# Talking-heads attention in pipelined pairs of tiles, and FiLM biases, on one Trainium2 core: the second mixing two pairs behind, three pairs of mixed scores, biases added by VectorE

## The reference, cut to what matters

```python
dots = jnp.einsum('bhid,bhjd->bhij', q, k) * scale        # k, v: 16 memory rows, then the tokens
dots = jnp.einsum('bhij,hk->bkij', dots, pre_proj)        # first mixing
dots = jnp.where(causal[None, None], neg, dots)
vk = lax.top_k(dots, 64)[0][..., -1:]
dots = jnp.where(dots < vk, neg, dots)
attn = jax.nn.softmax(dots, axis=-1)
attn = jnp.einsum('bhij,hk->bkij', attn, post_proj)       # second mixing
out = jnp.einsum('bhij,bhjd->bhid', attn, v)
return out.transpose(0, 2, 1, 3).reshape(b, n, h * d) @ Wo + bo
```

```python
scale_in, shift_in = jnp.split(c_t @ W_film_in + b_film_in, 2, axis=-1)
x = x * (1.0 + mod_gate * scale_in) + mod_gate * shift_in
y = s4d(x, ...)
scale_out, shift_out = jnp.split(c_t @ W_film_out + b_film_out, 2, axis=-1)
y = y * (1.0 + mod_gate * scale_out) + mod_gate * shift_out
```

## Time and profile before

| | us |
|---|---|
| Median of 3 timed runs (lowest, highest) | 4224.01 (4220.88, 4232.35) |
| The profiled execution, its own time | 4254.16 |
| Its span | 4252.3 |
| Busy in the span: PE, DVE, ACT, POOL | 3085.7, 2504.3, 1066.9, 967.3 |
| `l1_attention`, from the first search to the last reciprocal (1179 to 2713) | 1534 |
| `modulate` (from 2987.5) | 53 |
| `convolve` (3056.8 to 3233) | 176 |

### The profile page before, as it was taken

The page is one execution under the profiler, slowest core; times in us unless marked ns, Lnnn a source line. Parts: engine busy times, 40 slices in busy tenths (PEclk is TensorE's granted clock), DMA queues, the critical chain, the costliest instruction groups (busy, mean ns, idle before and its releaser), DMA issues. The chain is left out here.

```text
span 4252.3 us, 41618 instructions
## 1 busy us (share of the span) xinstructions
PE 3085.7 (73%) x12160; PEld 1887.1 (44%) x12160; DVE 2504.3 (59%) x7782; ACT 1066.9 (25%) x2741; POOL 967.3 (23%) x1212
## 2 busy tenths in 40 slices
PE   4747973997576777777677765443797855999997
PEld 2324552775343454455345444321233532555554
DVE  5994654551359989997999899568433141111112
ACT  1114531341133333333334332211001110111111
POOL 2540003002034544444444444200220000000000
PEclk6558986998657868767777866765898956999999
DMA  2000004554122122111212111000100003000000
GB/s 78 0 0 15 4 18 167 165 162 133 55 81 73 45 74 65 63 59 59 74 44 77 49 58 30 25 5 0 53 0 20 3 2 99 0 0 0 0 0 20
DMA packets 158964, 199.66 MB, mean 47 GB/s; under 512 B 30750, under 2 KB 133731, under 8 KB 158758
## 3 DMA queue, kind: packets, MB, share of 16 engines
q1 hardware_dynamic: 155686, 188.85, 14.1%
q0 software_dynamic: 3072, 8.39, 0.6%
HBM read 136.12 MB, written 61.08 MB: 46 GB/s over the span
## 5 line engine op out<-in xcount | busy, mean ns | idle before, releaser
L2058 DVE MATCH_REPLACE8 a_rest<-a_best,a_rest 128x416 f32<-128x416 f32 (+54 forms) x1308 | 605.0, 471 | 0.0
L2066 DVE MAX8 a_best<-a_rest 128x8 f32<-128x416 f32 (+54 forms) x1308 | 566.3, 475 | 0.0
L1736 PE MATMUL a_pmix<-a_rows,a_kpre 128*128 128x264 f32 (+41 forms) x528 | 244.7, 606 | 380.0 <-ACT a_mixed L1860 375.3
L2000 POOL TENSOR_SCALAR a_probs<-a_mixed,a_best 128x120 f32<-128x120 f32 (+12 forms) x208 | 285.7, 1373 | 377.5 <-DVE a_best L2070 354.2
L2843 DVE TENSOR_TENSOR e_hT<-e_act_out,e_pc 128x512 f32<-128x512 f32 x128 | 88.0, 687 | 478.4 <-ACT e_act_out L2834 472.8
L1736 PEld LDWEIGHTS a_pmix<-a_rows,a_kpre 128*128 128x128 f32 x528 | 123.7, 274 | 431.0 <-issue 423.6
L1745 PE MATMUL a_pat<-a_kp,a_probs 128*128 128x128 f32 x1344 | 261.2, 361 | 53.4 <-POOL a_kp L1962 48.5
L1745 PEld LDWEIGHTS a_pat<-a_kp,a_probs 128*128 128x128 f32 x1344 | 235.0, 262 | 126.7 <-POOL a_kp L1962 73.1
L2797 PE MATMUL e_ph<-xT,e_w 128*128 x512 | 244.4, 600 | 55.8 <-PEq L2760 46.7
L1726 PE MATMUL a_psc<-a_kT,branch 64*128 64x264 f32 (+3 forms) x640 | 234.8, 641 | 27.4 <-ACT a_stage L1827 26.6
L2814 PE MATMUL e_py<-e_w,e_hT 128*128 128x256 f32 x1024 | 254.4, 391 | 0.0
(11 more groups left out here) (448 smaller groups left out, 5608.0 us busy)
## 6 DMA issues: line engine op xcount, KB each, us to landing
f_w<-in_L_ffn_W SPq DMA_DIRECT2D x39, 1024.0 KB, 5.8
l_scores<-a_stage SPq DMA_DIRECT2D x32, 528.0 KB, 2.7
l_scores<-a_stage SPq DMA_DIRECT2D x32, 400.0 KB, 2.4
l_scores<-a_stage SPq DMA_DIRECT2D x32, 272.0 KB, 2.1
f0o_w<-in_L_ffn_W SPq DMA_DIRECT2D x8, 1024.0 KB, 12.5
sorted_x<-z_blank SPq DMA_DIRECT2D x1, 4992.0 KB, 17.1
f_xs<-sorted_x SPq DMA_DIRECT2D x39, 128.0 KB, 5.4
sorted_y<-f_ys SPq DMA_DIRECT2D x39, 128.0 KB, 5.7
```

The source lines that it names most:

```text
L1736: ins = pe.matmul(pmix[:, at, 0:hi - lo], kpre[:], rows[:, g % 4, lo:hi], start=True, stop=True)
L2000: ins = pool.tensor_scalar(p, x, best[:, a, LAST, 7:8], HIDE, ALU.is_lt, ALU.mult)
L2058: last[a] = signal(dve.match_replace(rest[:, a, 0:wd], best[:, a, q - 1, :], rows_of[a] if q == 1 else rest[:, a, 0:wd], GONE))
L2066: last[a] = signal(dve.max(best[:, a, q, :], rest[:, a, 0:wd]))
```

## The change

In `l1_attention`:

- `mixed` becomes a ring of six tiles (`DEEP`), three pairs; every index into it changes, and `mixed_out` waits for the mask of the tile six before.
- ACT's iteration k is now: mixed_out(k + 1) of both tiles, exps(k - 1), negated(k) of both, side(k), post_out(k - 2), products(k).
- `post`, `post_out`, `weights` and `invert` are now two pairs behind the search (k - 2); the loops of PE and ACT run one iteration longer. POOL's weights stand before the zeroing of `probs`.
- `heads` start one iteration later in a group, and the last iteration of a group has two of them; those of the very last group stand behind an extra iteration.
- The memory's values are no longer added by matmul. SP reads them from DRAM once a batch straight into `v`, after it has waited for two copies of values, and the first head product of a group waits for that (`mem_in`).

In the film stages the bias is read broadcast to 128 rows, `offset`, and made once into gate times bias, plus 1 in the left half. The one-row matmuls go, and one `scalar_tensor_tensor` of 512 columns (PSUM times gate plus `offset`) stands for the two `tensor_scalar` of 256.

```diff
-        return [(n, j) for j in range(8)] if s == 0 else []
+        return [(n, j) for j in range(8)] if s == 1 else []
...
-    return [(n, s)]
+    return [] if s == 0 else [(n, s - 1)] if s < STEPS1 - 1 else [(n, s - 1), (n, s)]
...
-        mixed = sb("mixed", [P, 4, KEYS1])
+        mixed = sb("mixed", [P, DEEP, KEYS1])
...
+                    if k >= 0 and (pos, s) == (1, 0):
+                        sp.wait_ge(sc_read, fills_to(("v", b, 1)))
+                        sp.dma_start(v[0:MEM, 0, :].rearrange("m (h d) -> m h d", h=H1),
+                                     d["L1_attn_mem_v"].rearrange("h m d -> m h d")).then_inc(mem_in, 16)
...
-                    if c == 0:
-                        ins = pe.matmul(out[:], G.ident[0:MEM, :], mv[:, half], start=False, stop=True)
...
-                        if k >= 1:
-                            post(2 * (k - 1) + a)
+                        if k >= 2:
+                            post(2 * (k - 2) + a)
...
-                for k in range(-1, PAIRS1 + 1):
-                    for a in range(2):
-                        if k >= 1:
-                            exps(2 * (k - 1) + a)
+                for k in range(-1, PAIRS1 + 2):
                     for a in range(2):
                         if k + 1 < PAIRS1:
                             mixed_out(2 * (k + 1) + a)
+                    for a in range(2):
+                        if 1 <= k <= PAIRS1:
+                            exps(2 * (k - 1) + a)
+                    for a in range(2):
                         if 0 <= k < PAIRS1:
                             negated(2 * k + a)
...
-                    if k >= 1:
-                        weights(k - 1)
...
-                        if q == min(rounds[0], TOP1 // 16) and pair >= 1:
-                            invert(pair - 1)
+                        if q == min(rounds[0], TOP1 // 16) and pair >= 2:
+                            invert(pair - 2)
+                invert(PAIRS1 - 2)
                 invert(PAIRS1 - 1)
...
+                sp.dma_start(offset[:], d["L1_xattn_b_film_in"].partition_broadcast(P)).then_inc(loaded, 16)
...
+                step(dve.tensor_scalar(offset[:], offset[:], gate[:, 0:1], None, ALU.mult))
+                step(dve.tensor_scalar(offset[:, 0:D], offset[:, 0:D], 1.0, None, ALU.add))
...
-                    dve.tensor_scalar(s1[:, i % 2], pw[i % 2][:, 0:D], gate[:, 0:1], 1.0, ALU.mult, ALU.add)
-                    ins = dve.tensor_scalar(h1[:, i % 2], pw[i % 2][:, D:2 * D], gate[:, 0:1], None, ALU.mult)
-                    ins.then_inc(emptied, 1)
+                    dve.scalar_tensor_tensor(film[:, i % 2], pw[i % 2][:], gate[:, 0:1], offset[:], ALU.mult, ALU.add
+                                             ).then_inc(emptied, 1)
...
-        pe.matmul(out[:], cT[:, k, i * P:(i + 1) * P], w[:, k, :], start=(k == 0), stop=False)
-    return pe.matmul(out[:], ones[:], bias[:], start=False, stop=True)
+        ins = pe.matmul(out[:], cT[:, k, i * P:(i + 1) * P], w[:, k, :], start=(k == 0), stop=(k == KD - 1))
+    return ins
```

More of the change, by code:

```diff
@@ L1435 @@
 PAIRS1 = GROUPS1 * STEPS1
+DEEP = 6
 def l1_group(n):
@@ L1712, in values @@
                         x = xv[:, k, :] if c == 0 else G.xT[:, k, at:at + rows_]
-                        ins = pe.matmul(out[0:rows_, :], x, w[:, k, half], start=(k == 0), stop=(c > 0 and k == KD - 1))
-                    if c == 0:
-                        ins = pe.matmul(out[:], G.ident[0:MEM, :], mv[:, half], start=False, stop=True)
+                        ins = pe.matmul(out[0:rows_, :], x, w[:, k, half], start=(k == 0), stop=(k == KD - 1))
                     full(ins)
@@ L1802, in wide @@
                     return 0 <= k < PAIRS1 and l1_tile(2 * k)[3] > BANK
-                for k in range(-2, PAIRS1 + 1):
+                for k in range(-2, PAIRS1 + 2):
                     if wide(k + 1):
@@ L2308, in modulate @@
         w = sb("w", [P, KD, 2 * D])
-        bias = sb("bias", [1, 2 * D])
-        ones = sb("ones", [1, P])
+        offset = sb("offset", [P, 2 * D])
+        film = sb("film", [P, 2, 2 * D])
         g = sb("g", [P, D])
@@ L2336, in _ @@
                         pe.wait_ge(emptied, i - 1)
-                    film_product(pe, pw[i % 2], cT, w, ones, bias, i).then_inc(full, 1)
+                    film_product(pe, pw[i % 2], cT, w, i).then_inc(full, 1)
             @block.gpsimd
@@ L2378, in convolve @@
         w = sb("w", [P, KD, 2 * D])
-        bias = sb("bias", [1, 2 * D])
-        ones = sb("ones", [1, P])
+        offset = sb("offset", [P, 2 * D])
+        film = sb("film", [P, 2 * D])
         skip = sb("skip", [P, D])
```

81 lines of the change are left out of this document (38 added, 43 removed).

## The result

| | before | after |
|---|---|---|
| median, us (runs) | 4228.2 (4 runs, 4220.9 to 4232.9) | 4167.6 (4 runs, 4161.2 to 4171.8) |
| ratio, 95% interval | | 0.986, 0.984 to 0.988 |
| profiled execution: own time, span, us | 4254.2, 4252.3 | 4168.5, 4166.6 |
| attention, first max to last reciprocal, us | 1533.2 | 1496.4 |
| attention, last reciprocal to the next stage's first operation on DVE, us | 22.3 | 24.7 |

What follows compares the result with a forecast made beforehand. DVE's top-64 search was taken to bound layer 1's attention, PE the film stages. Attention 27 us plus film 30 made 57, subtracted from the median 4224.0: 4167 us, range 4140 to 4196 for 8 in 10.

Steps and rivals of the forecast that it cites:

- wide turns: Attention, turns from a widest group to the next narrow one: both DVE waits go, 21 us gained in all.
- narrow turns: Attention, turns into the next batch's narrowest group: most waits stay, 1 us gained a turn, 3 in all; ceiling 22 a turn.
- first four pairs: Attention's start, paced by PE: fifth iteration about 5 us earlier, masks give 1 back; 4 us gained (2 to 8).
- short waits: Attention, scattered short waits of DVE: they go, 2 us gained.
- end of the stage: Attention's end: two post-mixes now come after the last search; costs 3 us (2 to 4).
- modulation: Film stage: 2.3 us a tile beside POOL for 9.4 tiles, then 1.92 for 6.6; 13.6 us gained.
- convolution: Film stage bound by PE: 16 pairs of bias passes of 1.05 us go, 16.8 us gained.
- broadcast loads: Both film stages: the bias broadcast to 128 partitions may land later, 0.4 us lost twice, 0.8 in all.
- the deadline moves from the middle of pair k to its end: Attention: the reciprocal of exponentials k-1 is needed later, as pair k+1 still waits for negated(k); 6.3 us a wide turn.
- Rival 1: Attention: all turn waits vanish, as six mixed buffers let DVE run through; 63 us more, 4104 us; chance 0.07.
- Rivals 2 and 3: 2: POOL's compares wait for PE's post-mixes, attention gains nothing, 4194, chance 0.15; 3: that loop bounds wide pairs, 4237, 0.03.
- rival 3: Attention: that loop outlasts the search and bounds all 64 wide pairs; 70 us lost, 4237 us; chance 0.03.

Runs made afterwards that it cites:

- `ring_only`: Kernel after with post-mix, weights, reciprocal and head products back at one pair behind, six rows and new order kept; ratio 0.988 to the kernel before.
- `heads_off`: Kernel after with the older group's output product and the head products moved out of the four pairs of a narrow turn; ratio 0.9784 to the kernel before.
- `neg_first`: Kernel after with ACT doing pair k's negated maximum ahead of the exponentials of pair k-1; ratio 0.984 to the kernel before, attention stage 1496.4 us.
- `mod_nogain`: Kernel after with POOL's gain and bias work in the modulation cut to one column of each tile; that stage took 38.2 us against 43.8.
- `film_only`: Kernel before with only the film stages (modulation, film product, convolution) of the kernel after; ratio 0.9925 to the kernel before, 32 us faster.
- `after_again`: Kernel after, unchanged, measured a second time beside the kernel before; ratio 0.9851, 59 us faster by medians.
- `attn_only`: Kernel before with only the attention of the kernel after, film stages left; ratio 0.9918 to the kernel before, 35 us faster.

## Why the prediction was right, point by point

| term, us gained | predicted | traces of after (2nd) | step |
|---|---|---|---|
| wide turns | 21 | 21.5 (18.9) | right |
| narrow turns | 3 | 9.9 (7.6) | too small by 5 to 7, inside its own ceiling |
| first four pairs | 4 | 3.3 (3.6) | right, by two sizes that offset |
| short waits | 2 | 2.3 (2.2) | right |
| end of the stage | -3 | -2.4 (-2.3) | right; 0.7 to 2.5 by trace |
| modulation | 13.6 | 16.6 | three sizes off |
| convolution | 16.8 | 18.6 | one size off |
| broadcast loads | -0.8 | -1.7 | one size off |
| experts of layer 1, untouched | 0 | -9.4 (-7.6) | not foreseen |
| sum | 57 | 59 (56) | medians: 60.6 (58.7) |

**The wide turns.** The step "the deadline moves from the middle of pair k to its end" is shown by `ring_only` (the first wait stays without the lag), and "PE can run both projections some 5 us earlier" by the second wait, which the order alone shortens. In the trace they start 10.4 us earlier against T's first max (1.33 us before it instead of 9.03 behind), and PE then waits 5.17 us for POOL's weights; the exponentials of T end 14.8 us behind that max, 14.4 predicted. What I didn't see is that the order is what carries the lag: without it the kernel would be slower than before.

**The narrow turns.** The mechanism was right (5.81 and 10.27 us stay, of 5.72 and 11.34), the balance of 1 us wasn't. I let the 16 passes of post(T-1) take back in the next iteration what the shorter post gave. In the trace they take 2.05 us, inside DVE's wait of 3.58, and pairs T+3 and T+4 got shorter (3.44 to 2.64 and 4.63 to 3.57). A likely cause is that head products start a step later; no run tests it by itself. The ledger says 3.3 us a turn (2.5 in the second profile); `ring_only` has 1.8 of them. That the ceiling was not in reach was rightly argued: the output product was the hold (18.5 us, `heads_off`), and the negated maximum one of two (`neg_first`).

**The first four pairs.** The fifth pair begins 3.5 us earlier (5 predicted), and the wait for the masks gives 0.2 back (1 predicted), so 4 came out near 3.3 by two errors that offset.

**Rival 1** was excluded for the right reason. By the Trainium skill (Perfetto Trace Analysis, section "Identifying Performance Opportunities"), the same gap repeating on the saturated engine can mean too few buffers. Here the traces show another cause: the kernel after has six rows and keeps the gaps at the narrow turns (5.81 and 10.27 us), with the old order six rows instead of four gave 1618.8 us against 1619.2, and what filled 18.5 us of the gaps was the place of an output product.

**Rivals 2 and 3** are real mechanisms that the kernel after escapes by its order. The wait of compares for post-mixes is 21.8 us on POOL (12.5 on line 2003, 9.3 on line 2001; 13.9 in before), and it reaches DVE in one place, 7.50 us in the first batch. The price that I gave the loop in rival 3 (70 us for all wide pairs) is near what it cost where it closed (86 against before), but by chance: it lost at the turns and in the last pairs before them, not in every wide pair.

**The modulation.** "DVE needs 2.3 us a tile beside POOL" was 2.48 (2930.94 to 2950.75 for eight tiles), as the products took 0.85 to 0.97 and 0.83; the prediction's own three sizes, 0.74, 0.95 and 0.83, add up to 2.52 and not to 2.3. Two others erred the opposite way. 2.97 less 1.05 isn't PE's period without a bias; 1.72 is, and DVE caught up at 1.58. And 9.4 and 6.6 tiles are 16 periods, where from the first film operation to the last there are 15: the trace has nine (21.81 us) and six (9.68 us). The film operation took 0.742 us, 0.74 predicted. `mod_nogain` shows the split: 5.6 us are left to POOL. By the Trainium skill (SBUF — State Buffer, section "SBUF: two separate sides"), DVE and GpSimd lock their shared ports against each other for an operation's whole length, on DVE's side by operations with two SBUF inputs or in a fast mode that uses both ports. The trace agrees: an operation with one input from PSUM stays at 0.74, the products fall from 0.85 to 0.97 back to 0.42 without POOL, and the `tensor_scalar` that adds 1 to the scaled bias, SBUF to SBUF, takes 0.70 us beside POOL's columns and 0.29 without.

**The convolution.** I took 1.05 us a pair of bias passes, the modulation's row; the convolution's own row says 17.9 us for 32, so 1.12, and the sum of that row was the better term. 18.6 us went, of which 0.4 were lost again at the load.

**The sum.** The stages that the change touches gained 68 us in the traces (64 in the second), 7 to 11 more than predicted; that the medians say 60.6 is in part luck. Layer 1's experts, untouched, took 713 to 715 us in the profiles of `film_only`, the kernel after and `after_again`, 709 in those of `attn_only` and `heads_off`, and 703 to 706 in the nine others. PE's granted clock accounts for it. At each of the stage's three changes of batch PE stands idle for 3.0 to 3.1 us in every trace. In the three long ones the clock then fell to 0.50 for 6.8 us each time; in before it fell once, for 3.4 us. Over PE's whole stretch in the stage that is 26.3 to 26.7 us at 0.50, against 15.0 in the two middle ones and 6.3 to 9.2 in the short ones. The stretch, and five us behind the same change of batch, in before and in after (length; PE, PEld, DVE, ACT, POOL busy; PE clock; DMA share, GB/s):

```profile
3570.00:4228.00 658.00, 648.74 (x2176) 379.18 (x2176) 92.22 (x140) 114.94 (x164) 0.00 (x0) 1.00 0.00 0
3903.00:3908.00 5.00, 5.00 (x13) 1.74 (x12) 1.35 (x2) 1.39 (x3) 0.00 (x0) 1.00 0.00 0
```

```profile
3476.00:4142.00 666.00, 651.05 (x2144) 381.69 (x2176) 92.27 (x140) 115.05 (x164) 0.00 (x0) 0.98 0.00 0
3811.00:3816.00 5.00, 4.64 (x6) 1.71 (x8) 0.35 (x1) 1.35 (x2) 0.00 (x0) 0.50 0.00 0
```

Why the clock falls behind the same idle time in one execution and not in another stays open, and so does whether it goes with the kernel or with the execution, as each kernel has one trace and the kernel after two.

## What to carry to other kernels

Two edits to a loop over four engines can't be priced one by one: write down the round (who waits for whom, back to the start), and see which edge each edit opens. A lag added without the edge opened made this kernel slower than it was. Where a wait's releaser has been moved away, look for the second one that stands right behind it on another engine's queue before promising the gain. And of an engine's passes that go from every tile, take the row of the stage itself, and the period that the rest can run at, not a difference of periods from a stretch where another engine held it. Last, lay the untouched stages of two traces side by side before comparing totals: here two of them moved by 28 and 9 us.

## What was not expected of the hardware

Beside a busy POOL a `tensor_scalar` of 256 columns within SBUF took 0.70 us instead of 0.29; it has one tensor input, and my prediction counted only operations with two as stretched. Four matmul passes of 512 columns have a period of 1.72 us in this stage, and two bias passes with one row cost 1.25 us a tile there (2.97 less 1.72), not less than two full ones (0.86). Behind the same 3.0 us of idle time PE's granted clock fell to 0.50 in some traces and stayed at 1.00 in others, worth up to 9.4 us in one stage of untouched code.
